# A four-batch decoder layer on one core: float32 products of the first two batches cut into three float32r products

## The reference, cut to what matters

```python
x = x + mixer(layernorm(x));  x = x + attention(layernorm(x), ctx);  x = x + moe(layernorm(x))

def mixer(x):                       # x: 4 x 512 x 512, d_inner 1024, 16 heads, 16 states
    xn = x * rsqrt(mean(x*x) + eps) * w_norm
    proj = einsum('bld,td->blt', xn, W_in)        # z 1024 | xi 1024 | dt 16 | B 256 | C 256
    xi = silu(causal_conv4(xi));  dt = softplus(dt + dt_bias);  dA = exp(dt * A)
    u = dt * mean_over_head(xi) * B
    h_t = dA_t * h_(t-1) + u_t;  y_t = sum(h_t * C_t)          # scan over the 512 tokens
    y = (y @ W_h2i.T) * silu(z)
    return y @ W_out.T + x
```

## Time and profile before

| | us |
|---|---|
| median of 3 runs (1219.15 to 1223.37) | 1219.8 |
| the profiled execution's own time | 1216.94 |
| its span in the profile | 1215.1 |
| PE busy in the span | 1168.5 (96%) |
| DVE / ACT / POOL busy | 691.5 / 475.3 / 386.6 |
| granted TensorE clock, share of full | 0.999 |

### The profile page before, as it was taken

How to read it: one execution, slowest core, us unless ns; L and a number is a source line. 1 busy time by engine, 2 the same in 40 slices (tenths; PEclk the granted TensorE clock), 3 DMA queues, 4 the chain that set the end, 5 groups by cost and what they waited for, 6 DMA issues and landing times. The chain is left out here.

```text
span 1215.1 us, 31305 instructions
## 1 busy us (share of the span) xinstructions
PE 1168.5 (96%) x13185; PEld 581.4 (48%) x13186; DVE 691.5 (57%) x1150; ACT 475.3 (39%) x669; POOL 386.6 (32%) x502
## 2 busy tenths in 40 slices
PE   6999999999999999999999999999999999999997
PEld 3444434444545544545645554444444444444443
DVE  3833595756787665668675777877657222222221
ACT  3320324533555453545453455555632222222222
POOL 5212311221321330231122121110102576777775
PEclk9999999999999999999999999999999999999999
DMA  8321874104384201364500245200135676678640
GB/s 205 103 80 32 190 161 120 29 15 120 69 162 85 72 25 28 84 118 105 112 20 16 68 105 93 83 3 3 72 114 166 171 188 138 142 225 233 182 83 2
DMA packets 119603, 122.24 MB, mean 101 GB/s; under 512 B 25472, under 2 KB 84992, under 8 KB 119344
## 3 DMA queue, kind: packets, MB, share of 16 engines
q1 hardware_dynamic: 101744, 98.59, 31.6%
q0 software_dynamic: 17008, 21.16, 9.0%
q10 hardware_dynamic: 720, 0.61, 0.2%
HBM read 94.63 MB, written 40.77 MB: 111 GB/s over the span
## 5 line engine op out<-in xcount | busy, mean ns | idle before, releaser
L683 DVE TENSOR_REDUCE mx<-ps_m 128x2 f32<-128x1024 f32 x256 | 313.0, 1223 | 193.6 <-PE ps_m L1024 189.3
L892 ACT ACTIVATE prob<-ps_s 128x1024 f32<-128x1024 f32 x256 | 262.0, 1023 | 322.7 <-PE ps_s L1024 321.7
L1024 PE MATMUL acc<-xnT,wring 128*32 128x512 f32 x1888 | 249.0, 592 | 0.6 <-DVE first_z L619 0.6
L1869 PE MATMUL ps_gu<-ring,xgT 128*128 x376 | 176.7, 593 | 1.0 <-DVE xgT L1573 1.0
L1508 POOL DMA_INDIRECT out<-y,dest x92 | 143.7, 1562 | 77.5 <-ACT y L1734 60.4
L1024 PE MATMUL ps_s<-q_stack,k_stack 99*32 99x512 bf16 x2048 | 161.7, 380 | 4.4 <-ACT prob L892 3.8
L1024 PE MATMUL ps_m<-k_stack,q_stack 96*32 96x512 bf16 x1952 | 153.2, 380 | 9.8 <-DVE mx L683 8.2
L1573 DVE COPY xgT<-ps_x 128x512 f32<-128x512 f32 x47 | 32.5, 692 | 202.1 <-PE ps_x L1839 202.1
L1209 PE MATMUL ps_o<-prob,values 128*32 128x128 f32 x4096 | 138.4, 273 | 0.0
L1209 PEld LDWEIGHTS ps_o<-prob,values 128*32 128x32 f32 x4096 | 116.3, 110 | 44.7 <-issue 39.2
L1024 PEld LDWEIGHTS ps_m<-k_stack,q_stack 96*32 96x32 bf16 x1952 | 55.6, 96 | 127.3 <-issue 72.8
(11 more groups left out here) (282 smaller groups left out, 1201.6 us busy)
## 6 DMA issues: line engine op xcount, KB each, us to landing
ring<-in_w_experts SPq DMA_DIRECT2D x96, 256.0 KB, 4.7
wring<-in_w_in SPq DMA_DIRECT2D x80, 256.0 KB, 4.2
q_stack<-part_rows SPq DMA_DIRECT2D x96, 128.0 KB, 4.6
wring<-in_w_out SPq DMA_DIRECT2D x32, 256.0 KB, 2.9
part_rows<-part SPq DMA_DIRECT2D x20, 384.0 KB, 3.8
out<-x SPq DMA_DIRECT2D x4, 1024.0 KB, 4.8
xt<-in_x SPq DMA_DIRECT2D x14, 256.0 KB, 4.6
k_stack<-part_rows SPq DMA_DIRECT2D x48, 64.0 KB, 3.0
```

The lines of the kernel that those rows point to most:

```text
L683: nc.vector.tensor_reduce(mx[:, n % G, 2 * u:2 * u + 2], ps_m[:, :, :], AX.X, ALU.max).then_inc(s_max, 1)
L892: nc.scalar.activation(prob[:, slot % PROB, :, :], ps_s[:, :, :], ACT.Exp, scale=SCALE).then_inc(s_exp, 1)
L1024: ins = nc.tensor.matmul(dst[c:c + 32, :], stationary[:, c:c + 32], moving, start=start, stop=stop, tile_position=(0, c))
L1869: ins = nc.tensor.matmul(ps_gu[p][:, :], xgT[:, p, k * P:(k + 1) * P], weights(own)[:, k * 2 * F:(k + 1) * 2 * F], start=(k == 0), stop=(k ...
```

## The change

For batches 0 and 1 each float32 operand is cut into a high piece, rounded to float32r, and a low piece, the exact remainder. A product of two operands is then high x high + high x low + low x high, three float32r matmuls in place of one float32 matmul. This holds for the 20 blocks of batches 0 and 1 and for batch 0's `project_out`; the dt columns stay float32 products, of both pieces. The pieces are made at run time: ACT copies `raw` weights to the high piece (28 times), POOL subtracts (28 times); SP stores each pair of pieces (512 KB) to DRAM and batch 1 loads 20 of them again. Tokens: ACT and DVE, 16 small instructions each for a batch, in place of four larger ones on DVE. Gated values of batch 0: ACT, then DVE (even) or POOL (odd), before `project_out`. Batch 0 takes the xi blocks first (1 to 8), then B and C (9 to 12), and its `head_means` stands at step 22, `outputs` at step 32; the statistics of batch 1's tokens move to step 24 and behind. Between slot 0 and slot 13 matmuls other than the attention's own tiled ones are no longer cut in four (`FULL_SLOTS`). The ring of probabilities shrinks from 6 to 4.

```diff
-    RING = 10
+    RING = 5
+    RAW = 10
-    PROB = 6
+    PROB = 4
-    Y_AT = (40, 38, 38, 38)
+    Y_AT = (32, 38, 38, 38)
+    XI = (1, 5, 5, 5)
+    BC = (9, 1, 1, 1)
+    MEANS_AT = (22, 30, 30, 30)
+    NEXT_AT = (24, 4, 4, 4)
+    ORDER = (0, 2, 4, 6, 1, 3, 5, 7)
+    SPLIT_BATCHES = 2
+        FULL_SLOTS = PERIOD * (SPLIT_BATCHES - 1) - LEAD + 2 * GROUPS
+        SPLIT_AT = {w: consumed(0, w - RING)[2] for w in range(RING, PIECES)}
+        LOW_AT = {w: at + 1 for w, at in SPLIT_AT.items()} | {17: 31, 18: 32, 24: 50}
+        X1_AT = ((59, 60, 61, 62), (50, 54, 58, 62), (50, 54, 58, 62), (50, 54, 58, 62))
...
+            def store_pieces(w):
+                sp.wait_ge(s_wlow, w + 1)
+                sp.dma_start(dram["w_pieces"][w], pieces[:, w % RING, :, :].bitcast(F32)).then_inc(s_wst[w % RING], 16)
+                if w + RAW < PIECES:
+                    load_raw(w + RAW)
...
+            def low_weights(w):
+                pool.wait_ge(s_whigh, w + 1)
+                nc.gpsimd.tensor_tensor(pieces[:, w % RING, 1, :], raw[:, w % RAW, :], pieces[:, w % RING, 0, :],
+                                        ALU.subtract).then_inc(s_wlow, 1)
...
+            def evacuate_low(b, j):
+                dve.wait_ge(s_xhigh, TB * b + j + 1)
+                turned = four[j] if b == 0 else ps_t[:, :]
+                for k in range(KD):
+                    cols = slice(j * P, (j + 1) * P)
+                    ins = nc.vector.scalar_tensor_tensor(
+                        out=xnT_low[:, k, cols], in0=turned[:, k * P:(k + 1) * P], scalar=wnorm[:, k, 0:1],
+                        in1=xnT_high[:, k, cols], op0=ALU.mult, op1=ALU.subtract)
...
+            def high_weights(w):
+                act.wait_ge(s_raw[w % RAW], 16 * (w // RAW + 1))
+                if w >= RING:
+                    done, value, _ = consumed(0, w - RING)
+                    act.wait_ge(done, value)
+                    act.wait_ge(*stored(w - RING))
+                nc.scalar.activation(pieces[:, w % RING, 0, :], raw[:, w % RAW, :], ACT.Copy).then_inc(s_whigh, 1)
...
+            def split_product(dst, stationary, moving, start, stop):
+                nc.tensor.matmul(dst, stationary[0], moving[0], start=start, stop=False)
+                nc.tensor.matmul(dst, stationary[0], moving[1], start=False, stop=False)
+                return nc.tensor.matmul(dst, stationary[1], moving[0], start=False, stop=stop)
...
-                tiled[0] = slot >= 0
+                tiled[0] = slot >= FULL_SLOTS
```

468 lines of the change are left out of this document (314 added, 154 removed).

## The result

The changed kernel takes 1222.49 us (median of 20 runs, 1219.6 to 1226.64), the kernel before 1219.94 in the same session: ratio 1.0024, 95% interval 1.0015 to 1.0033. The interval excludes 1, so it is slower, by less than the 0.5% that the prediction took as its bound. The forecast of 1205 us was wrong, and 1222.49 lies just above its range (1194 to 1221). The profiled execution has a span of 1221.7 us, 6.6 more than that of before; the medians are 2.6 apart. From slot 17 to the end both traces take nearly the same (977.5 and 978.1 us), so what follows is about the first 244 us.

The account below looks back on a forecast made before the run. PE was taken to bound batch 0's projections, output products and 186 to 230 us, DVE 155 to 186; -5.3 - 7.0 + 0.9 + 0 - 3.5 = -14.9 us on 1216.94 gives 1202, as median about 1205, range 1194 to 1221.

Parts of the forecast that it names:

- The unit: PE's float32r matmul of 512 columns: 0.215 us each, three taking 0.644 us in place of a float32 product's 0.858.
- rival of a float32 record's price: A float32r matmul costs 0.429 us like a float32 record, giving 1250 to 1290 us; chance 0.09.
- a weight load which does not fit: A load not fully hidden makes each matmul 0.25 us, 12 us lost, 1213 to 1222 us; chance 0.06.
- The start: Up to batch 0's first block: dt begins at 15.5 us as now, first block at 17.5 for 16.45; 1 us lost.
- Seven silus and eight taps take 22.6: DVE's xi chain in batch 0: taps start at 24.1 us, last silu done at 47.0; PE waits 2.6 us before head_means.
- The round of the gain: Batch 0, from head_means' end to the last csb: 20.5 us in place of 15.9, ready at 69.5 us.
- Hidden by DVE's pace: Batch 0's DMA of pieces: 2.3 us a block, under DVE's 2.82, so it costs nothing.
- my DMA rival: DMA or ACT bounds batch 0: 3 us lost and up to 5 more, 1208 to 1213, or 1220 us; chance 0.15.
- The wait before `outputs`: PE reaches batch 0's outputs at 60.6 us, the gain is ready at 69.5: a wait of 8.9 us.
- Gates and output products: Batch 0's gates and output products: 32 x 0.215 us saved, 7 us gained.
- I cost them at nothing: Additional pieces of batch 0's gated values are covered at no cost; without cover, 1.3 us for each late piece.
- Slots 1 to 13: 26 half steps save 5.6 us, less 1.1 for changes of matmul form at 0.14 each and up to 1: 3.5 gained.

Follow-up runs that it names:

- e5_extra_narrow: Changed kernel plus three float32r matmuls of 128 columns, each with its own weight load, in each step of batch 0's blocks; one run, 1234.65 us.
- e2_cut_late: Changed kernel with POOL's five head weight cuts moved behind xi's last silu and SP's copies behind the gain's rows; 1220.96 us, ratio 1.0009.
- e12: e9 with small float32 products into an unused bank ahead of batch 0's heads_to_inner matmuls; 1209.0 us, ratio 0.9912.
- e4_no_stores: Changed kernel without weight piece stores except block 0's (others 32 bytes), all loads kept, batch 1 computed from wrong weights; 1219.92 us, ratio 1.0005.
- e3_pe_kept_busy: Changed kernel with 11 float32 products of 512 columns into an unused bank just ahead of batch 0's outputs; 1219.69 us, ratio 1.0003.
- e10: e9 with float32 products into an unused bank before batch 0's head means, outputs and each heads_to_inner; 1207.54 us, ratio 0.9895.
- e13: e9 with the scores and maxima of slots 0 to 13 cut in four again; 1213.76 us, ratio 0.9957.
- e9: Changed kernel with cuts, five loads, ones memset, scans, outputs and value copies later, POOL's two csb together ahead of a low piece; 1207.9 us, ratio 0.9911.
- e7_scans_later: Changed kernel with DVE's scans behind z's first three silus, POOL's bsb behind batch 1's power, csb and outputs later; 1216.77 us, ratio 0.9974.

## Why the prediction was wrong

**The unit** was mis-sized by 8%: 0.233 us in place of 0.215 (for a bfloat16 product the rows gave 0.22, 0.44 for two, which I took for 0.215). On 336 matmuls of batch 0 that is 6.2 us of PE's work, of which only the parts that PE bounds count. The rival of a float32 record's price was wrong, and that of a weight load which does not fit is refuted as a cause by e5_extra_narrow, though its number (0.25, 1213 to 1222) was the nearest of all.

**The start** (1 us forecast lost, 4.2 measured at the first block). I took DVE "behind" ACT and the power by pairs as a gain. POOL's memset beside the normalisation cost 1.5 us of it; putting it elsewhere brought dt 0.9 us sooner. And dt itself took 3.6 us (17.05 to 20.65) instead of 2: its records lie twice as far apart as those of batch 1's dt, which takes 1.9 us (131.53 to 133.47). That looks like the half clock behind a wait of 3.0 us, but the profile gives 1.00 as the granted clock of 17 to 20 us, so the cause is not shown.

**"Seven silus and eight taps take 22.6"**, the xi chain on DVE, is the first step that failed. The durations came from a trace in which POOL was idle. Beside POOL's unbroken low pieces and cuts the silus took 1.31 us in the mean instead of 0.68, and the chain from the first tap to the last silu took 27.9 us (25.71 to 53.62) in place of the 22.9 forecast. e2_cut_late turned this back: silus of 0.86 us in the mean, a chain of 24.2 us, `head_means` 3.8 us sooner. The other 2.8 of the 6.6 us by which `head_means` was late are PE's own, the late start and the unit, for in e2_cut_late PE goes into it without a wait. That the wait before it came out at 2.6 us as forecast is chance: PE and DVE were both 6.6 us late. A page of the Trainium skill, "SBUF — State Buffer", section "Who interferes with whom", says that a DVE instruction with two SBUF inputs contends with a POOL instruction that reads SBUF, and that of two such instructions the first keeps the shared ports to its end while the other blocks. The trace agrees in kind: 0.68 became 1.47 to 3.90, taps with a PSUM operand kept 2.31. It does not agree in degree: as I read the page the loser waits for one instruction, while at 40.43 it waited for two and in e12 for the remainder of five.

**The round of the gain** (10.9 us to `bsb`, measured 13.7; 20.5 in all, measured 23.7). I priced SP's queue (2 us; e4_no_stores gives 1.9) and left the transfer itself at its old length. e4_no_stores shows 4.2 us of the 13.7 to be the traffic of the pieces, queue and transfer together. "Hidden by DVE's pace" held for the blocks and not for the gain's rows, which have to pass through the same DMA engines; my DMA rival had "up to 5 more as the gain's rows go through a full queue" in it, on the wrong side of an "or".

**The wait before `outputs`** was forecast at 8.9 and measured at 9.9. Here the mechanism was right. What I left out is what a wait does to PE: behind it `outputs` took 2.8 us and the first matmuls lay 0.43 apart, as if at half the clock:

```profile
79.86 3.78 PE L1229 MATMUL ps_t<-csb,state_sum 128*128 128x512 f32 x4 [9.88 <-POOL csb L678]
82.65 1.42 PE L1237 MATMUL acc<-xnT_high,pieces 128*128 128x512 f32 x1
83.86 0.63 PE L1238 MATMUL acc<-xnT_low,pieces 128*128 128x512 f32 x1
84.29 0.63 PE L1239 MATMUL acc<-xnT_high,pieces 128*128 128x512 f32 x1
```

The granted clock of 70 to 80 us is 0.60, and 0.72 behind. e3_pe_kept_busy gives its price, 2.8 us from `outputs` to the end of block 20.

**Gates and output products** (7 us forecast, 2.5 measured: 33.1 us from `heads_to_inner` to dt against 35.6, where 28.6 was forecast). "I cost them at nothing", of the additional pieces, held in this execution, though DVE's and POOL's pieces stretch each other (2.88 us for two): the first output product follows the first `heads_to_inner` by 5.8 us, before by 6.2, and behind it PE's longest wait is 0.35 us. (In e12 the same term cost 5.6 us.) What failed are the products. 1.8 of the 4.5 us are the unit, and 2.4 the clock, 0.66 from 100 to 110 us: from the first output product to dt it is 27.3 us, in e10, at 1.00, 24.9. Why the clock falls here is open. The kernel before has gaps of 0.2 to 1.2 us between these matmuls as well, and its clock stays at 1.00.

**155 to 186 us: nothing** was right. From dt to slot 0 the stretch lost 1.2 us (60.5 us against 59.3), where "into batch 1" had forecast 0.9.

**Slots 1 to 13** (3.5 us forecast, 1.6 measured: 45.1 us from slot 0 to 14 against 46.7). Half steps save 0.15 us, 3.9 in all. A change of the matmuls' form out and back costs 0.29 us (e13), not 0.14. Six slots with `products` pay it and save next to nothing (from slot 5 to 6 before 3.68, after 3.56, while from 4 to 5 it is 2.60 and 2.29); batch 1's head means pay it too. Seven of them are 2.0 us, so 1.9 should be left of the 3.9, and some 0.3 us stay unassigned.

The sum: the spans are 21.5 us off. Batch 1's dt is 18.7 of it: 6.6 at the start of `head_means`, 0.6 in `head_means` at the lower clock, 3.2 in the round up to `outputs` (23.7 against 20.5), 2.8 by the clock behind the wait, 1.1 by the unit in five blocks and 4.5 at the gates and output products. The stretch up to slot 0 adds 0.3, slots 1 to 13 add 1.9, and what lies behind slot 14 the last 0.6. Undone one at a time the causes move dt by 3.7 (POOL's cuts), 4.6 (stores), 3.5 (kept busy in the wait) and 7.5 (scans and their wait behind z's silus); these overlap, since each also shortens what the others act on. Undone by order, in e9, they and the wait itself move it by 16.1. That e9 comes out near the forecast of 1205 is in part chance: it has no wait of 8.9 us, which the forecast had, and a slower unit, which it had not.

## What to carry to other kernels

A saving on the busiest engine is worth what the shortest cover behind it allows: look at every round trip that was just hidden (here 15.9 us hidden but for 0.24) and ask which queue, bank and program order stands behind its first late result, because moving the waiting instruction alone only moves the wait. Durations read beside an idle POOL are lower bounds: work added to POOL without pauses stretches DVE's instructions with two SBUF operands by up to its own length. And a change that fails by waits can often be mended by order alone: moving a few instructions within their engines' orders, with no less work, took 1.1% (14 us) off. Before a start is compared between two traces, look whether a weight load stands ahead of it without its matmul: read from the first `heads_to_inner` record that is there, e3_pe_kept_busy would gain 1.8 us at that point and not 3.4.

## What had not been expected of the hardware

- A DVE instruction with two SBUF operands can wait for several POOL instructions in a row: 3.90 us behind two, 6.48 behind the remainder of five, in place of 0.68. Where POOL pauses 1.5 us between its steps, it takes 0.68.
- A float32r matmul of 512 columns takes 0.233 us, one of 128 columns with its own weight load 0.11. Two bfloat16 products took 0.44.
- A long wait of PE costs twice: the granted clock was 0.60 in the stretch of the 9.9 us and 0.72 in the next, in which matmuls lay 0.43 instead of 0.23 us apart. Short gaps can do the same: at the gates, with PE busy 5.70 of 10 us, the next stretch had 0.86 (e9). They need not: behind the wait of 2.6 us before `head_means` the clock fell to 0.50 in the kernel after and stayed at 1.00 in e7_scans_later. What decides is not shown.
- Matmuls cut in four between whole ones cost 0.29 us for each change out and back (e13).
